# A graph layer with sort, gather and feed-forward on one core: sort keys of half degrees, the sort in one run, lists from the second step, weights centred later

## What is computed

```python
xn = _layernorm(x)
xp = (xn @ W).reshape(n, 4, 64)
a_src = einsum('nhc,hc->nh', xp, att_src); a_dst = einsum('nhc,hc->nh', xp, att_dst)
alpha = leaky_relu(a_src[src] + a_dst[dst], 0.2)          # edges and one self loop per node
w = softmax of alpha over the edges of each dst
out = elu(segment_sum(xp[src] * w, dst) + bias)
```

## Time and profile before

| what | us |
|---|---|
| median of 3 executions (3161.61 to 3163.52) | 3163.41 |
| the profiled execution, its time | 3166.19 |
| its span, first to last instruction | 3164.4 |
| pass over x, about | 31 to 316 |
| 98 scatters on POOL | 220.0 to 345.2 |
| gathers on POOL begin | 358.0 |
| POOL busy over the span | 2108.6 (67%) |
| PE busy | 2127.0 (67%) |
| DVE busy | 1910.4 (60%) |

### The profile page before, as it was taken

The page is one execution under the profiler, slowest core; times in us unless marked ns, Lnnn a source line. Parts: engine busy times, 40 slices in busy tenths (PEclk is TensorE's granted clock), DMA queues, the critical chain, the costliest instruction groups (busy, mean ns, idle before and its releaser), DMA issues.

```text
span 3164.4 us, 38617 instructions
## 1 busy us (share of the span) xinstructions
PE 2127.0 (67%) x8271; PEld 1510.3 (48%) x8271; DVE 1910.4 (60%) x4819; ACT 732.8 (23%) x2199; POOL 2108.6 (67%) x2189
## 2 busy tenths in 40 slices
PE   4557358877766676667767677777764366269998
PEld 3435135544444444444545454555443111168887
DVE  7996458877777777755555555555555688742221
ACT  2225232211111111121112111122210366222222
POOL 4727667777777777777777777777773688044433
PEclk7669679988888888788888888888877677579999
DMA  5537644444444444455555555555543699211111
GB/s 169 155 108 229 114 112 124 128 123 124 124 124 124 125 125 127 132 145 153 153 153 153 153 153 153 155 153 153 152 130 88 171 291 292 82 34 56 55 55 45
DMA packets 259969, 426.67 MB, mean 135 GB/s; under 512 B 73682, under 2 KB 165748, under 8 KB 259764
## 3 DMA queue, kind: packets, MB, share of 16 engines
q0 software_dynamic: 96592, 260.07, 31.7%
q1 hardware_dynamic: 163300, 165.80, 16.5%
HBM read 337.21 MB, written 88.48 MB: 135 GB/s over the span
## 4 chain that ended last, share of the span: by engine, by line
POOL 37%; issue 20%; PE 19%; DVE 16%; DMA 4%; ACT 1%; ACTq 1%; DVEq 1%; POOLq 1%; SPq 0%
POOL G L1234 31%; PE bank L2033 7%; PE bank L916 5%; PE bank L925 5%; DMA G<-tab_d,sidx 4%; POOL rows_d L1218 3%; POOL G L1211 3%; DVE G L1645 2%; DVE G L557 1%; DVE G L553 1%; DVE G L554 1%; DVE acc L1661 1%; DVE G L538 1%; ACT sidxF L1858 1%; ACTq L1854 1%
## 5 line engine op out<-in xcount | busy, mean ns | idle before, releaser
L1234 POOL DMA_INDIRECT G<-tab_d,sidx x1632 | 1549.2, 949 | 518.0 <-issue 479.9
L2033 PE MATMUL bank<-G,ident 128*128 128x264 f32 x3264 | 920.8, 436 | 600.7 <-DVE G L1645 519.7
L2033 PEld LDWEIGHTS bank<-G,ident 128*128 128x128 f32 x3264 | 656.9, 212 | 861.8 <-issue 515.3
L1645 DVE TENSOR_TENSOR G<-G,bank 128x1024 f32<-128x1024 f32 x408 | 491.1, 1214 | 1.8
L1661 DVE TENSOR_TENSOR acc<-acc,bank 128x264 f32 x816 | 347.8, 426 | 193.7 <-PE bank L2033 160.9
L1900 ACT ACTIVATE bank<-work 128x196 f32<-128x196 f32 x51 | 17.2, 338 | 1210.7 <-DVE work L1632 1210.7
L2014 PE MATMUL bank<-kvw,shared 128*128 128x512 f32 x392 | 183.7, 613 | 48.6 <-DVE shared L1563 36.7
L1616 DVE CAST work<-penI 128x64 f32 (+1 forms) x51 | 11.7, 229 | 321.4 <-DMA G<-tab_d,sidx 318.3
L1984 PE MATMUL bank<-G,acc 128*128 128x264 f32 x392 | 136.4, 507 | 95.3 <-DVE acc L1374 73.1
L889 POOL DMA_INDIRECT out<-G,acc x49 | 48.9, 998 | 192.5 <-DVEq L1004 182.9
L916 PE MATMUL bank<-G 128*128 128x256 f32 (+1 forms) x800 | 175.4, 378 | 0.0
(11 more groups left out here) (398 smaller groups left out, 3118.0 us busy)
## 6 DMA issues: line engine op xcount, KB each, us to landing
G<-tab_d,sidx POOLq DMA_INDIRECT x1632
acc<-x_in SPq DMA_DIRECT2D x98, 256.0 KB, 4.0
shared<-xnT_d SPq DMA_DIRECT2D x98, 256.0 KB, 3.9
accP_d<-acc SPq DMA_DIRECT2D x100, 132.0 KB
tab_d<-acc SPq DMA_DIRECT2D x49, 260.0 KB, 3.3
xnT_d<-acc SPq DMA_DIRECT2D x49, 256.0 KB, 2.3
mix_d<-acc SPq DMA_DIRECT2D x49, 256.0 KB, 3.0
G<-mix_d SPq DMA_DIRECT2D x49, 256.0 KB, 4.3
```

What stands on the lines that cost most here:

```text
L1234: g.indirect_dma_start(out=G[:, s, t, 0:TR], out_offset=None, in_=tab_d, in_offset=bass.IndirectOffsetOnAxis(ap=sidx[:, s, t:t + 1], axis= ...
L1645: v.tensor_tensor(gm[:, q4], gm[:, q4], W1[:, q4][:, :, :, None].to_broadcast([P, 4, HG, CG]), ALU.mult).then_inc(g_ready, 1)
L2033: last = te.matmul(bank[1 + i % NSB][:, 0:ROW], ident[:, :], G[:, s, i * IT + k, :], start=(k == 0), stop=(k == IT - 1))
```

## The change

It does four things. The keys are made of half the degree, rounded up (`itemsI`, two more small instructions), so that there are `KB` = 40/2 + 2 = 22 of them and the one-hot array has 22 x 98 = 2156 elements; the number of items of a block is then the count of keys itself, and three small instructions of `place_nodes` go. `list_edges` stands in steps 1 to 14 in place of 4 to 17. `degrees`, `keys`, `count_keys`, `place_nodes`, `rank_keys` and `positions` all stand in step 15, `item_ends` in 17 and `item_blocks` in 19; PE's three small products stand together behind `turn` of step 15. `centre` moves from step 1 to step 40.

```diff
     IC = CT // IT
-    KB = W + 2
+    KB = W // IT + 2
     MAXT = n_edges // P + 1 + W + 2 * NB
...
     HT = 4
-    LIST_AT, SORT_AT = 4, 18
+    LIST_AT, SORT_AT, CENTRE_AT = 1, 15, 40
     FLAT = (0, 16, 32, 48, 64, 80, NB)
     DUMMY = float(NPAD)
-    assert NKA == 2 and NK0 == 5 and len(FLAT) == 7
+    assert IT == 2 and NKA == 2 and NK0 == 5 and len(FLAT) == 7
     assert NB == 2 * NP and NP % 2 == 1 and NQ % 2 == 1 and n_edges <= EP and NB % GB == 0 and NB > FLAT[-2]
...
         iota_k = apiece(KB)
-        oneh = apiece(KB * NB)
-        csum = apiece(KB * NB)
-        under = csum[:, 0:SJ * P // 2].bitcast(BF16).rearrange("p (j n) -> p j n", j=SJ)
+        sort_a, sort_b = apiece(max(KB * NB, 2 * NT)), apiece(max(KB * NB, SJ * P // 2))
+        oneh, csum = sort_a[:, 0:KB * NB], sort_b[:, 0:KB * NB]
+        under = sort_b[:, 0:SJ * P // 2].bitcast(BF16).rearrange("p (j n) -> p j n", j=SJ)
         Send = apiece(KB + 1)
...
         kcmp = apiece(KB)
-        nbI = apiece(2).bitcast(I32)
+        itemsI = apiece(NB).bitcast(I32)
         nbB = apiece(P)
...
         ao[0] += ao[0] % 2
-        pr = oneh[:, 0:2 * NT].bitcast(I32).rearrange("p (t k) -> p t k", k=2)
+        pr = sort_a[:, 0:2 * NT].bitcast(I32).rearrange("p (t k) -> p t k", k=2)
         pr_end = apiece(2).bitcast(I32)
...
                 lk(v.tensor_scalar(deg[:, lastcol], deg[:, lastcol], valid_last[:, :], None, ALU.mult))
-                lk(v.tensor_scalar(key, deg, -1.0, float(KB - 1), ALU.mult, ALU.add))
+                lk(v.tensor_scalar(itemsI, deg, float(IT - 1), None, ALU.add))
+                lk(v.tensor_scalar(itemsI, itemsI, 1, None, ALU.arith_shift_right))
+                lk(v.tensor_scalar(key, itemsI, -1.0, float(KB - 1), ALU.mult, ALU.add))
                 lk(v.tensor_scalar(key, key, 0.0, None, ALU.max))
...
             onesS, lowS = bank[0][:, 256:256 + KB + 1], bank[0][:, 320:320 + KB + 1]
-            p128, kcount, lanes, nbF, mxd = (bsmall[:, i:i + 1] for i in range(5))
+            p128, _, lanes, nbF, mxd = (bsmall[:, i:i + 1] for i in range(5))
             endc = bsmall[:, 5:6]
...
                 lk(v.tensor_scalar(p128, pcol[:, :], float(P), None, ALU.mult))
-                lk(v.tensor_scalar(kcmp[:, 0:W], onesS[:, 2:KB], p128, None, ALU.is_gt))
-                lk(v.tensor_reduce(kcount, kcmp[:, 0:W], AX, ALU.add))
-                lk(v.tensor_scalar(nbI[:, 0:1], kcount, 1.0, None, ALU.add))
-                lk(v.tensor_scalar(nbI[:, 1:2], nbI[:, 0:1], 1, None, ALU.arith_shift_right))
-                lk(v.tensor_copy(nbF, nbI[:, 1:2]))
+                lk(v.tensor_scalar(kcmp[:, 0:W // IT], onesS[:, 2:KB], p128, None, ALU.is_gt))
+                lk(v.tensor_reduce(nbF, kcmp[:, 0:W // IT], AX, ALU.add))
                 lk(v.tensor_scalar(lanes, pcol[:, :], float(NB), None, ALU.is_lt))
...
                 events.setdefault(LIST_AT + k, []).append((list_edges, k))
-            for at, f in ((0, degrees), (1, keys), (2, count_keys), (3, place_nodes), (3, rank_keys), (3, positions),
-                          (5, item_ends), (7, item_blocks)):
+            for at, f in ((0, degrees), (0, keys), (0, count_keys), (0, place_nodes), (0, rank_keys), (0, positions),
+                          (2, item_ends), (4, item_blocks)):
                 events.setdefault(SORT_AT + at, []).append((f, None))
...
                     table_rows(q)
-                if q == 1:
+                if q == CENTRE_AT:
                     dve.wait_ge(ld_kv, 32)
...
 
-            steps = {SORT_AT: next_starts, SORT_AT + 2: bin_starts, SORT_AT + 3: block_starts, SORT_AT + 5: blocks_of_items}
+            steps = {SORT_AT: (next_starts, bin_starts, block_starts), SORT_AT + 2: (blocks_of_items,)}
             turn(0, 0)
...
                     turn(q + 1, (q + 1) % 2)
-                if q in steps:
-                    steps[q]()
+                for step in steps.get(q, ()):
+                    step()
             pe.wait_ge(xr_ready, NP)
```

## The result

The changed kernel takes 3155.69 us (median of 12 executions, 3151.2 to 3158.38) against 3163.29 us for the kernel before in the same session (12 executions, 3160.71 to 3164.65). The ratio is 0.9975 with a 95% interval of 0.9968 to 0.9982: faster by 5.7 to 10.1 us, 7.6 in the middle. The forecast was 4.5 us, with a range that holds the result. But by the bound of 0.2%, 6.3 us, which the prediction set for "no change", the result lies just on the far side, where it had put 0.27 and not 0.66.

What follows compares the result with a forecast made beforehand. POOL's saturated gathers bound the kernel, so their start decides: landing at 346.5 now against ACT at 342.0 gives 4.5 us, though the pass ends 2.6 us later. 3163.4 - 4.5 = 3158.9 us, range 3151 to 3166.

Steps and rivals of the forecast that it cites:

- What bounds the kernel: POOL's saturated gathers, 500 to 2400 us: whatever starts them earlier by some us ends the kernel earlier by as much.
- Windows and lists: Before the sort: `list_edges(0)` starts at 45.01, POOL's 8.7 us gap goes, windows landed at 161.0, step 15 starts at 166.8.
- The sort in one run: Step 15 on DVE: `keys` starts at 170.6, the parts take 22.5 us, `pos_i` at 193.1, 26.7 us before 219.8.
- The pass behind it: Step 16 to the end: `centre` in step 40 costs 10.0 us, pass ends at 318.8, 2.6 us later than now.
- What starts the gathers: Hand-over to gathers: ACT's keys and values at 342.0, after scatters landed at 328.9; stage starts 4.5 us earlier than now.
- A: Pass not lengthened, as windows suffer less or PE's clock returns sooner: gain 7 to 12 us, about 3154; chance 0.24.
- B: At the gathers' start, the scatters' lead counts in full: 17.6 us, 3146; chance 0.03.
- C: Slower: `centre`'s pause in the pass leaves PE at the low clock level longer, up to 3172.7; chance 0.06.
- D: In the gathers, merged keys cost a chunk: 32 gathers at 1.25, 40 us, 3199; chance 0.01.
- The scatters: No backlog: the last two groups wait for `row_ready` of pairs 46 and 49, first at about 309.6; landed at 328.9.
- the prediction's signs: Right if: 13 groups of scatters, then gaps before the last; `pos_i` near 193; ACT's last root near 342 without landing wait.
- What was costed at nothing: Behind the gathers' start: 51 chunks stay, register loads and copies of the lists follow ACT as now.

Runs made afterwards that it cites:

- the last four: Sort spread, centring in step 1: 3142.92 us; same, ACT's register loads first: 3137.69; changed kernel, register loads first: 3148.22; changed kernel, centring in six parts: 3148.87.

## Why the prediction was right, point by point

- **What bounds the kernel.** Right. The run of the changed kernel with the register loads first, in which nothing but ACT's stretch before the list was shortened, brought all of it to the end.
- **Windows and lists.** Right: the windows landed for the last list at 160.9, forecast 161.0. The run with the centring in step 1 has the same `pos_i`, so the windows and not DVE set it.
- **The sort in one run.** Right: `pos_i` at 192.9, forecast 193.1. The bridge that needed a choice, PE's products without cover, was 1.43 and 1.20 us of waiting, forecast 1.5 and 1.3.
- **The pass behind it.** The mechanism was right, the size off, and this is the term of the sum that was mis-sized. From the start of step 16 to step 25 it took 229.99 - 192.91 = 37.1 us, forecast 39.1, and the centring cost 7.2 us (313.7 against the 306.5 of the kernel without it), forecast 10.0. Both prices were read from the one pause of the earlier trace rows, behind which PE stayed at 0.50 for 9.2 us, two projections. Here one projection was slow behind `item_blocks`, and one behind the longer pause of the centring. The pass ended at 313.7, forecast 318.8. How many are slow is partly luck: of the ten traces of the table, all with the same `item_blocks`, four have two and six have one. With a second one the pass would have ended some 2 us later and the gain come out nearer to the forecast (an estimate, from the 5.01 us in place of 3.22 of that step in the kernel before).
- **What starts the gathers.** Right in kind: ACT's root and not the landing. The chain from the end of the pass to the root took 24.6 us, forecast 23.2 by the row of before, since PE's eight products for the second pair took 5.13 us, at a granted clock of 0.72, in place of 3.70 at 1.00. The two errors are of opposite sign: 5.1 less 1.4, so that the list should have come 3.7 us before the forecast, and it did (8.45 against 4.5 us, 0.25 us of it in the loads).
- **Rivals.** A is what happened, in its mild form and by its second condition, that PE's clock comes back sooner than in the earlier trace rows: its gain of 7 to 12 us holds the 7.6, and it had 0.24. So the range held the result, but the likeliest outcome, a gain below 6.3 us, did not come. B is excluded by the first list, which waited for ACT and not for the landing. C did not happen: the three traces of the table with the whole centring in step 40 have one slow projection behind it each. D did not: 1632 gathers in each.
- **The scatters.** The thirteenth group began at 308.2 (forecast 309.6) and the last row landed at 327.1 (328.9). The gaps stood before the twelfth and thirteenth group, where the prediction's signs had them before the last; it changed nothing, since the landing was not the later event.
- **What was costed at nothing.** The register loads ran behind the root as said. That they were themselves on the path was in the text, though not as something to take away.

## What to carry to other kernels

When a stage starts at the later of two chains, a gain on one is worth only the slack of the other; read the slack before the gain. In this kernel 7.7 us of work, moved out of a stage that another engine bounds into one paced by a chain of waits, cost 7.1 us in one piece and 0.2 us in six parts, each about as long as the idle time of a step. Before a difference of some us between two traces is put down to an edit, look for where in the pass it arises: 2 us of several pass ends here arose ahead of the edited step. Test the parts of a change one by one even when the whole is faster: here one part alone (the keys) was better than the whole, and another (the moves) worse than nothing.

## What the runs showed of the hardware

The saturated stage of 1632 gathers, from the first issue to the last, took 2053.4 us in the profile of before, 2050.6 with the change, and 2048.6 (moves alone), 2048.8 (centring in step 1), 2053.2 (keys alone), 2053.7 (centring in step 48) and 2048.8 to 2049.5 (the last four) in the others. It follows neither the number of keys nor the places of the sort. So about 3 of the 11.5 us between the two profiled spans are this spread, and a single profile of this kernel cannot tell differences of less than 5 us.

A pause of PE of 4.6 us brought a low stretch of 9.2 us, two projections. The same instructions, with pauses of 4.6 to 4.9 us, brought one slow projection in six traces and two in four, and the pauses of 6.0 to 6.5 us behind the whole centring brought one in all three. Behind the pass, the eight matmul records of 128 x 512 of the first pair took 5.09 us (granted clock 0.72) to 6.58 us (0.56), and those of the second 3.70 us (1.00) to 5.40 us (0.68), in ten traces. The clock's return is the least predictable term of this stretch, by some 2 us at each of these places.

In one set of runs all kernels took 30% longer with waits called "remote"; what these are stays open.
